# Layer 1 of a graph network on one core: gathered rows of 320 columns, one operand of two VectorE operations in PSUM, and the next group's scores between two pairs of adds

## What is computed

```python
s_u = x @ W_u.T + b_u                      # 8 scores of a node as source
s_v = x @ W_v.T                            # 8 scores of a node as destination
e = s_u[src] + s_v[dst]
e = jnp.where(e >= 0, e, 0.2 * e)
m = jax.ops.segment_max(e, dst, num_segments=n_nodes)
e_exp = jnp.exp(e - m[dst])
denom = jax.ops.segment_sum(e_exp, dst, num_segments=n_nodes)
probs = e_exp / denom[dst]
msg = x.reshape(n_nodes, 32, 8)[src] * probs[:, None, :]
out = jax.ops.segment_sum(msg, dst, num_segments=n_nodes)
```

## Time and profile before

| | us |
|---|---|
| runs before | 4690.83, 4700.78, 4711.7; median 4700.78 |
| the profiled execution | 4686.26 |
| its span, first to last instruction | 4684.5 |
| first to last `take_scores` of layer 1 (54 groups) | 3262.39 to 4579.72 |
| busy of the whole span | POOL 3468.7, PE 3095.6, DVE 2213.4, ACT 908.4 |

### The profile page before, as it was taken

One profiled execution on the slowest core, in us unless ns is written; L12 is line 12 of the kernel. 1 busy time (PEld: TensorE's weight loads), 2 busy tenths in 40 slices (PEclk: granted clock), 3 DMA queues, 4 the chain that ended last, 5 costly groups with the idle time before them and its releaser, 6 DMA issues. The chain is left out here.

```text
span 4684.5 us, 61408 instructions
## 1 busy us (share of the span) xinstructions
PE 3095.6 (66%) x13554; PEld 1900.7 (41%) x13555; DVE 2213.4 (47%) x5019; ACT 908.4 (19%) x2810; POOL 3468.7 (74%) x2948
## 2 busy tenths in 40 slices
PE   2548777877777777777777776884545555555541
PEld 1224444444444444444444443552333333443331
DVE  2553333333333333333333332995766667766665
ACT  0212222222222222222222222332000000000002
POOL 4237888888888888888888886775777777777764
PEclk9768888889888888888889897996777767667765
DMA  8667666667666667666667666565443434444431
GB/s 300 168 235 176 125 132 134 133 126 138 129 133 125 133 131 135 124 133 130 135 125 131 133 133 132 177 202 172 115 113 109 113 113 114 114 112 114 114 102 63
DMA packets 471759, 641.52 MB, mean 137 GB/s; under 512 B 173607, under 2 KB 365635, under 8 KB 467886
## 3 DMA queue, kind: packets, MB, share of 16 engines
q0 software_dynamic: 198144, 339.26, 38.1%
q1 hardware_dynamic: 245994, 254.83, 18.2%
q10 hardware_dynamic: 27588, 47.08, 3.1%
HBM read 448.23 MB, written 192.71 MB: 137 GB/s over the span
## 5 line engine op out<-in xcount | busy, mean ns | idle before, releaser
L935 POOL DMA_INDIRECT S<-l_msum,l_sink x784 | 1284.8, 1639 | 254.2 <-issue 213.0
L1466 POOL DMA_INDIRECT l_feats<-X_rows,l_gsrc x880 | 1039.2, 1181 | 326.9 <-issue 264.6
L918 POOL DMA_INDIRECT l_ga<-A_rows,l_gsrc x784 | 789.7, 1007 | 265.6 <-issue 160.0
L1008 PE MATMUL l_psU<-l_hid,l_same 128*128 128x257 f32 x1568 | 585.9, 459 | 535.6 <-ACT l_hid L1044 505.3
L981 PE MATMUL l_psC<-l_table,l_onehot 128*128 x4728 | 727.4, 295 | 0.0
L1532 PE MATMUL l_psU<-l_feats,l_same 128*128 128x264 f32 x1760 | 553.5, 478 | 169.5 <-DVE l_feats L1701 124.6
L1048 ACT COPY l_msum<-l_psU 128x257 f32<-128x257 f32 x784 | 292.6, 373 | 1889.9 <-POOLq L934 1313.6
L974 PE MATMUL l_psC<-W1cT,l_attrT 64*128 64x256 f32 x1576 | 623.4, 479 | 13.0 <-DMA l_table<-B_rows 13.0
L981 PEld LDWEIGHTS l_psC<-l_table,l_onehot 128*128 128x128 bf16 x4728 | 426.1, 104 | 367.9 <-issue 306.0
L1008 PEld LDWEIGHTS l_psU<-l_hid,l_same 128*128 128x128 f32 x1568 | 267.4, 214 | 666.2 <-ACT l_hid L1044 579.0
L1532 PEld LDWEIGHTS l_psU<-l_feats,l_same 128*128 128x128 f32 x1760 | 409.0, 240 | 306.9 <-issue 216.8
(11 more groups left out here) (346 smaller groups left out, 3390.7 us busy)
## 6 DMA issues: line engine op xcount, KB each, us to landing
l_srcb<-src_rows SPq DMA_DIRECT2D x99, 512.0 KB
l_locb<-lo_rows SPq DMA_DIRECT2D x55, 512.0 KB
S<-su_zeros ACTq DMA_DIRECT2D x24, 1156.5 KB
l_locb<-loc_rows SPq DMA_DIRECT2D x99, 256.0 KB
nd_sums<-S SPq DMA_DIRECT2D x196, 128.5 KB, 2.2
l_attr<-in_edge_attr SPq DMA_DIRECT2D x98, 256.0 KB
GH_rows<-l_hidden SPq DMA_DIRECT2D x49, 384.0 KB
nd_hidden<-GH_rows SPq DMA_DIRECT2D x49, 384.0 KB, 3.1
```

The source lines that it names most:

```text
L918: pool.indirect_dma_start(ga[:, s, :], None, D["A"], bass.IndirectOffsetOnAxis(ap=gsrc[h][:, j % HALF:j % HALF + 1], axis=0)).then_inc(gat ...
L935: pool.indirect_dma_start(D[f"S{j % NTAB}"], bass.IndirectOffsetOnAxis(ap=sink[j // HALF][:, j % HALF:j % HALF + 1], axis=0), msum[:, j % ...
L1008: nc.tensor.matmul(psU[j % 2][:, 0:UW], same[j // HALF][:, j % HALF, :], hid[:, j % RING, :], start=True, stop=True).then_inc(agg_done, 1)
L1466: pool.indirect_dma_start(feats[r][:, t, :], None, D["X1"], bass.IndirectOffsetOnAxis(ap=gsrc[r][:, t:t + 1], axis=0)).then_inc(gathered[r ...
```

## The change

The rows of `X1` and of `feats` become 320 columns wide (1280 bytes); the 56 new columns are set to zero once, travel with every gather and are read by nobody. A pad of 24 floats ahead of `feats` puts the buffers on lines of 256 bytes. A new PSUM buffer `psW` holds a copy of `column` and the weights: `same` is now made of `column` in PSUM and `loX` in SBUF, and the multiplication takes the features from SBUF and the weights from PSUM. ScalarE takes the exponential twice, first into `psW` (VectorE waits for that) and then into `feats` (TensorE waits for that, with the new semaphore `weights_in_rows`). And on VectorE `take_scores` of the next group stands ahead of the adds 4 and 5, `local_max` between 5 and 6; on TensorE `turn_scores` stands behind pair 5.

```diff
+XR = 320
-        x1 = m.sb("x1", [P, UNR, XW])
+        x1 = m.sb("x1", [P, UNR, XR])
+            nc.vector.memset(x1[:, :, XW:XR], 0.0)
-        feats = [m.sb(f"feats{r}", [P, GROUP, XW]) for r in range(SETS)]
+        m.sb("align", [P, 24])
+        feats = [m.sb(f"feats{r}", [P, GROUP, XR]) for r in range(SETS)]
+        psW = m.ps("psW", [P, 512])
+        weight = psW[:, 0:GROUP * NH].rearrange("p (t h) -> p t h", h=NH)
+        column = psW[:, P:2 * P]
 # TensorE
                 pe.wait_ge(same_ready, g + 1)
+                pe.wait_ge(weights_in_rows, g + 1)
...
-                        i = nc.tensor.matmul(psU[n % 4][:, 0:XW], same[:, t, :], feats[r][:, t, :],
+                        i = nc.tensor.matmul(psU[n % 4][:, 0:XW], same[:, t, :], feats[r][:, t, 0:XW],
                     i.then_inc(agg_done, 1)
+                    if n == 5 and not last:
+                        turn_scores(g + 1, 1 - r)
                 if not last:
-                    turn_scores(g + 1, 1 - r)
                     gather_ends(g + 1)
 # ScalarE
-                nc.scalar.activation(feats[r][:, :, H:XW], below[:, :, :], ACT.Exp).then_inc(weights_ready, 1)
+                nc.scalar.activation(weight, below[:, :, :], ACT.Exp).then_inc(weights_ready, 1)
+                nc.scalar.activation(feats[r][:, :, H:XW], below[:, :, :], ACT.Exp).then_inc(weights_in_rows, 1)
 # VectorE
-                nc.vector.tensor_tensor(same[:, :, :], K["column"][:, :].unsqueeze(1).to_broadcast([P, GROUP, P]),
+                nc.vector.tensor_tensor(same[:, :, :], column.unsqueeze(1).to_broadcast([P, GROUP, P]),
...
+            nc.vector.tensor_copy(column, K["column"][:, :])
...
-                    w3 = f[:, :, H:XW].unsqueeze(2).to_broadcast([P, QUARTER, H // NH, NH])
+                    w3 = weight[:, q * QUARTER:(q + 1) * QUARTER, :].unsqueeze(2).to_broadcast([P, QUARTER, H // NH, NH])
                     nc.vector.tensor_tensor(f3, f3, w3, ALU.mult).then_inc(weighted, 1)
...
                 blocks = pair_words(g, 1)
-                add_sums(g, (4, 5, 6, 7), blocks)
                 if not last:
                     take_scores(g + 1, 1 - r, c)
+                add_sums(g, (4, 5), blocks)
+                if not last:
                     local_max(g + 1, 1 - r, c)
+                add_sums(g, (6, 7), blocks)
...
-    D["X1"] = dram("X1_rows", [NP, XW])
+    D["X1"] = dram("X1_rows", [NP, XR])
```

More of the change, by code:

```diff
@@ L1401, in layer1_phase @@
         max_ready, max_turned = m.sem("max_ready"), m.sem("max_turned")
-        below_ready, weights_ready = m.sem("below_ready"), m.sem("weights_ready")
+        below_ready, weights_ready, weights_in_rows = m.sem("below_ready"), m.sem("weights_ready"), m.sem("weights_in_rows")
         weighted, agg_done, acc_done = m.sem("weighted"), m.sem("agg_done"), m.sem("acc_done")
@@ L1697, in body @@
                 for q in range(4):
-                    f = feats[r][:, q * QUARTER:(q + 1) * QUARTER, :]
-                    f3 = f[:, :, 0:H].rearrange("p t (c h) -> p t c h", h=NH)
-                    w3 = f[:, :, H:XW].unsqueeze(2).to_broadcast([P, QUARTER, H // NH, NH])
+                    f3 = feats[r][:, q * QUARTER:(q + 1) * QUARTER, 0:H].rearrange("p t (c h) -> p t c h", h=NH)
+                    w3 = weight[:, q * QUARTER:(q + 1) * QUARTER, :].unsqueeze(2).to_broadcast([P, QUARTER, H // NH, NH])
                     nc.vector.tensor_tensor(f3, f3, w3, ALU.mult).then_inc(weighted, 1)
```

## The result

| | before | changed |
|---|---|---|
| median of the runs | 4702.8 us (4690.8 to 4711.7) | 5078.4 us (5077.1 to 5081.9) |
| ratio | 1 | 1.080 [1.077, 1.084] |
| profiled execution, span | 4686.3, 4684.5 us | 5077.3, 5075.5 us |
| layer 1, first to last `take_scores` | 1317.3 us, 24.4 a group | 1704.1 us, 31.6 a group |
| mean gather | 1188 ns | 959 ns |

A forecast was written before the change was run, and what follows sets the result against it. It took GpSimd's gathers, 23.8 us a group, as the bound. 54 groups of 21.6 us plus 24.4 make 1191 us against 1317.3; with 1 us for the node stage, 125 less: 4575 us, range 4520 to 4650.

The forecast's parts named there:

- Operands in PSUM, GpSimd's side: Layer 1 gathers: contention with `same` and the four multiplications goes, 3.6 us a group off GpSimd, leaving 20.2 us.
- VectorE at no cost: `same` and the multiplications: reading one operand from PSUM costs VectorE nothing; `same` stays at 2.28 us.
- Rival F: `same` and multiplications: VectorE reads the broadcast operand more slowly from PSUM; at twice the time 4964 us; chance 5%.
- rivals B and C: Gathers: B, part of the contention stays, up to 4613 us, 11%; C, operands change nothing for GpSimd, 4690 to 4700, 7%.
- The order: VectorE and TensorE chain in layer 1: the new order removes 1.6 us of VectorE's waits a group.
- TensorE's gap of 1 to 2 us ahead of pair 6: Sign expected in each layer 1 group: TensorE waits for the scores before pair 6, put at 1.2 us.
- Rival D: Pairs 6 and 7 on TensorE: waiting for scores costs the high clock, 1.8 us a group, 4674 us; chance 6%.
- A group of 21.2 to 21.95 us, mean 21.6: Layer 1 chain of VectorE and TensorE: 21.2 us where the clock rises early, 21.95 where late.
- rival E: Layer 1 chain is shorter than thought and GpSimd's 20.2 us is the bound: 4499 us; chance 5%.
- my sum: Layer 1 loop: 54 groups x 21.6 us + 24.4 us = 1191 us, against 1317.3 before.
- my 24.4 us: Two long layer 1 groups, 32.25 and 37.76 us, exceed two of 22.8 by 24.4 us, left in.
- the overlap: Layer 1 gathers run beside the chain, needing 20.2 of 21.6 us, and are in time by 3 us.

The follow-up runs named there:

- e2: The kernel before with both operands (column and the weights) in PSUM, rows of 264 columns and the old order: 5079.2 us, 1.082.
- e14: The changed kernel with 12 gathers a group in place of 16: 4803.5 us, 1.022.
- e15: The changed kernel with GpSimd paused behind its eighth gather of a group until the next group's maxima are turned: 5022.3 us, 1.068.
- e18: The changed kernel with a small memset behind each gather and GpSimd waiting for the memsets ahead of every fourth gather: 4849.5 us, 1.033.
- e17: The changed kernel with rows of 264 columns, no padding, and one more VectorE multiplication of 880 SBUF columns behind `same`: 5057.7 us, 1.075.
- e1_wide: The kernel before with rows of 320 columns and the 24 columns ahead of feats, nothing else: 4703.5 us, 1.001.

## Why the prediction was wrong

- **Operands in PSUM, GpSimd's side** (16 x 1.246 us, mean near 0.96): right, 959 ns on A and on E.
- **VectorE at no cost**: right for the two instructions, 2288 and 1215 ns. Rival F is out, and rivals B and C, since no contention with these instructions is left.
- **The order**: right as far as it could be seen. In a group on E TensorE's gap of 1 to 2 us ahead of pair 6 is 1.17 us, and the waits ahead of the adds and the scan are down to 0.34 and below. Rival D is out: the eight products behind the gap take 2.04 us, the high level.
- **A group of 21.2 to 21.95 us, mean 21.6**: on chip E the median is 22.0 and the largest 22.8. The adds 5 to 7 still wait 0.34, 0.20 and 0.27 us, of which I had allowed for 0.1; rival E, a shorter chain, is out. The loop there takes 1192.7 us and my sum was 1191, but that is luck: the mean group is 22.1 us, which makes 26 us more than I had, and no group is a long one, so my 24.4 us for these are not there. The two errors cancel.
- **The step that failed** is the overlap: "GpSimd needs 20.2 of 21.6 us. It is no longer the bound." I took the longer of the gathers and the chain for the group, and put what gathers that follow one another closely do to TensorE's reports at nothing. On A a group is the run of gathers, 2.8 us and 9.2 us, one behind the other: 31.6 us in the mean. The sign stood in another term, "I leave these 24.4 us in." Two groups of the kernel before lasted 32.25 and 37.76 us, I had no cause for them and carried them over as a constant. A piece of the longer one, of the kernel before:

```profile
4497.38 3.88 PE L1532 MATMUL l_psU<-l_feats,l_same 128*128 128x264 f32 x8 [3.59 <-DVE l_feats L1701]
...
4500.87 0.95 POOL L1466 DMA_INDIRECT l_feats<-X_rows,l_gsrc  x1 [0.30 <-issue]
4501.49 0.43 DVE L1611 TENSOR_TENSOR acc<-acc,l_psU 128x264 f32 x1 [1.78 <-PE l_psU L1532]
...
4505.76 0.43 DVE L1611 TENSOR_TENSOR acc<-acc,l_psU 128x264 f32 x1 [3.84 <-remote]
...
4507.12 0.95 POOL L1466 DMA_INDIRECT l_feats<-X_rows,l_gsrc  x1 [0.30 <-issue]
4508.56 0.43 DVE L1611 TENSOR_TENSOR acc<-acc,l_psU 128x264 f32 x1 [2.38 <-remote]
```

The last product ends by its record at 4501.26, and adds that need nothing else start at 4505.76 and 4508.56, while gathers follow one another at 0.95 us unstretched. It was there to be read: the three waits of over 3 us ahead of an add in this loop (4.36, 3.84 and 3.32 us) have no stretched gather beside them. It was a sign and no proof, since of the five of 2.0 to 2.9 us three do have one. Why this came up mainly in two groups, and at the adds rather than at `picked`, isn't known. The contention that the change removes was what kept the gathers apart. With it gone, nearly every group is a long one: on A, VectorE waits 51 times at `picked` and 8 times at `below`.

So the sum fits, by luck, where the reports are prompt, and where they are not it left out 31.6 - 21.6 = 10 us a group, 540 us (less the 24.4 that stood in it; against E's own groups the loss is 9.5 us). And I took three runs on one chip for the spread of the kernel.

What stands shown: the loss comes with the operands in PSUM and the second exponential alone (e2); the lateness ends when the run of gathers ends (e14: 5 us less run, 5 us less group), it follows the gathers and not the matmul or VectorE's PSUM reads (e15), the group is shorter with more holes between the gathers (e18), and it depends on the chip. The comparisons of e14, e15 and e18 with the changed kernel are between chips with late reports, not on one chip. The brake as I had it, one stretched gather behind `same`, fell (e17).

What is open: which path the reports share with the gathers, and what differs between the chips.

One rival is untested: the recording itself. Every timed run comes with a span and a granted clock, so none shows the kernel without any recording, and the two kinds of chip differ in the recording too. The traces of the changed kernel, alike in their 61519 instruction records, hold 43342 semaphore records on A, 45784 on D and 69893 on E; the twelve traces with late reports have 42434 to 45798, the eight others 69820 to 69941. So a delay that is worked out from semaphore records may be too long where one is missing; the starts of `picked`, which don't need them, give the same median of 9.3 us.

The data isn't it: on A the rows land 1.6 us after a gather's end from the first to the last of a run. Which operand alone would do it on a chip with late reports was not run, only the weights with the new order. No kernel is known to beat the others on both kinds of chip: of those run, the changed kernel is the fastest on E, and before on A, D, F, H and J, and on B, level with e1_wide.

## What to carry to other kernels

A stall that paces a stream may be what lets the rest work; before removing it, look for the few places in the trace where it happens to be missing, and see what they cost. An outlier that is left in a sum as a constant is a rival without a price. And where a kernel's waits end at nothing that can be their cause, time it on more than one chip before a forecast or a verdict is taken for the kernel's own.

## What the runs showed of the hardware

- Chips differ in kind, or in a state of theirs: in twelve traces from A, B, D, F, H and J some of TensorE's semaphores come late while gathers run (in the changed kernel on A `picked` starts up to 11.6 us after the small matmul's record ends); in eight traces from C, E and G the delay is 0.014 us but for one event. The chips without it also run the kernel before 0.8 to 1.6% faster.
- It isn't TensorE alone. Of VectorE's register operations in the changed kernel's loop on A, 138 of the 894 that begin beside a gather take over 0.4 us (at `same` 0.69 in the middle case) and 1 of the other 381; on E none of 1275 does. This adds the 36.5 us ahead of `same`. It is not the cause of the late reports: in e15_pause, which has them too, none of 1275 is slow. A load issued by SyncE in such a stretch takes up to 0.73 us, behind the run 0.34, and on E none takes over 0.38:

```profile
3902.53 0.73 SPq L1442 DMA_DIRECT2D l_locb<-lo_rows  x1
...
3940.28 0.34 SPq L1442 DMA_DIRECT2D l_locb<-lo_rows  x1
```

- A VectorE instruction of two SBUF inputs stretches a gather beside it (880 columns, 1.05 us: 1.57 us in place of 0.95); with one input in PSUM it does not, at 1024 and 2048 columns (mean gather 959 ns). The Trainium skill (SBUF — State Buffer, "Who interferes with whom") states the second. On the first it infers that a tensor_tensor leaves the making of descriptors alone, and the measured 1.57 us against 0.95 decides otherwise.
